# An output stage that starts inside the attention stage's block, with its tiles laid over the attention stage's

## What is computed

```
x1 = x  + 0.5 * ffn(layernorm(x))          # 1024x1024 weight, bias, LoRA terms
x2 = x1 + attn(layernorm(x1))              # latent attention, 32 heads, causal
y  = x2 + 0.5 * ffn(layernorm(x2))

attn: q    = rmsnorm(x @ wq_a.T) @ wq_b.T            # 32 heads of 64 + 64 (rope)
      ckv  = x @ wkv_a.T ; k_nope, v = rmsnorm(ckv[:64]) @ wkv_b.T
      p    = softmax(q @ k.T * scale, causal)
      out  = (p @ v).reshape(T, 32*128) @ wo.T
```

## Time and profile before

| | us |
|---|---|
| median of three runs | 1931.37 |
| the profiled execution | 1932.19 |
| its span in the trace | 1930.3 |
| TensorE busy | 1807.9 (94%) |
| VectorE busy | 1231.7 (64%) |
| ScalarE busy | 999.0 (52%) |
| GpSimd busy | 871.8 (45%) |
| mean granted TensorE clock | 0.981 |

### The profile page before, as it was taken

One profiled execution on the slowest core, in us unless ns is written; L12 is line 12 of the kernel. 1 busy time (PEld: TensorE's weight loads), 2 busy tenths in 40 slices (PEclk: granted clock), 3 DMA queues, 4 the chain that ended last, 5 costly groups with the idle time before them and its releaser, 6 DMA issues. The chain is left out here.

```text
span 1930.3 us, 44295 instructions
## 1 busy us (share of the span) xinstructions
PE 1807.9 (94%) x15472; PEld 1419.5 (74%) x15472; DVE 1231.7 (64%) x2653; ACT 999.0 (52%) x2135; POOL 871.8 (45%) x641
## 2 busy tenths in 40 slices
PE   6999959899999999999999999995799999968999
PEld 3678859777777777777777777773688888857887
DVE  5555348789888898888988888885421211125453
ACT  2211047788788887888878888783411100012210
POOL 2232112377787877878778787782000000014321
PEclk9999979999999999999999999998899999989999
DMA  6542153321222212222122221211742332225321
GB/s 225 173 159 103 55 166 97 83 64 41 84 68 67 77 41 84 68 67 71 46 84 67 67 68 50 84 63 62 256 131 87 103 115 87 66 109 175 120 88 65
DMA packets 111697, 182.48 MB, mean 95 GB/s; under 512 B 27472, under 2 KB 64464, under 8 KB 109584
## 3 DMA queue, kind: packets, MB, share of 16 engines
q1 hardware_dynamic: 111632, 181.61, 29.1%
HBM read 122.06 MB, written 59.51 MB: 94 GB/s over the span
## 5 line engine op out<-in xcount | busy, mean ns | idle before, releaser
L1040 PE MATMUL psS<-keyT,q 128*128 128x512 f32 (+2 forms) x2304 | 472.2, 350 | 24.5 <-POOL q L568 14.9
L1040 PEld LDWEIGHTS psS<-keyT,q 128*128 128x128 f32 x2304 | 380.5, 189 | 118.5 <-DVE negmax L1146 41.8
L1105 ACT ACTIVATE prob<-prob,negmax 128x640 f32<-128x640 f32 (+7 forms) x512 | 392.4, 769 | 77.7 <-DVE negmax L1146 75.0
L1156 DVE STREAM_TRANSPOSE pT<-prob 128x640 f32<-128x640 f32 (+7 forms) x512 | 380.0, 762 | 66.3 <-PE psV L1057 61.7
L1146 DVE CUSTOM_DVE_ANT_0 prob<-psS,mask 128x640 f32<-128x640 f32 (+7 forms) x512 | 371.8, 742 | 20.2 <-PE psS L1040 7.3
L419 PE MATMUL f_psy<-f_weff,f_xT 128*128 128x512 f32 x1344 | 313.8, 393 | 0.0
L1368 PE MATMUL o_psy<-o_w,o_o 128*128 128x512 f32 x1344 | 304.8, 389 | 0.0
L1368 PEld LDWEIGHTS o_psy<-o_w,o_o 128*128 128x128 f32 x1344 | 252.3, 188 | 52.3
L419 PEld LDWEIGHTS f_psy<-f_weff,f_xT 128*128 128x128 f32 x1344 | 250.9, 188 | 53.9 <-issue 1.7
L1057 PE MATMUL psV<-pT,val 32*64 32x512 f32 (+3 forms) x8192 | 265.8, 408 | 6.7 <-DVE pT L1156 6.2
L1057 PEld LDWEIGHTS psV<-pT,val 32*64 32x64 f32 x8192 | 169.1, 132 | 110.8 <-issue 67.2
(11 more groups left out here) (113 smaller groups left out, 1911.1 us busy)
## 6 DMA issues: line engine op xcount, KB each, us to landing
wo<-in_wo SPq DMA_DIRECT2D x16, 1024.0 KB, 6.0
pT<-row_scales SPq DMA_DIRECT2D x128, 128.0 KB, 2.8
oT<-pT SPq DMA_DIRECT2D x64, 256.0 KB, 2.5
o_in<-oT SPq DMA_DIRECT2D x32, 512.0 KB, 5.3
f_xt<-in_x SPq DMA_DIRECT2D x16, 512.0 KB, 4.3
f_w_in<-in_w SPq DMA_DIRECT2D x16, 512.0 KB, 6.6
w_sum<-f_w_in SPq DMA_DIRECT2D x16, 512.0 KB, 5.2
x<-f_xo SPq DMA_DIRECT2D x16, 512.0 KB, 2.9
```

The source lines that it names most:

```text
L1040: ins = nc.tensor.matmul(psS[:, slot, start + x0:start + x1], q[:, e, a, t * P:(t + 1) * P], k.keyT[:, m, b * S + x0:b * S + x1], start=(i ...
L1105: nc.scalar.activation(row, row, ACT.Exp, bias=negmax[:, n % 8:n % 8 + 1], scale=-1.0, accum_out=rowsum[:, column(n, s):column(n, s) + 1]) ...
L1156: nc.vector.transpose(pT[:, n % 2, t, 0:width], prob[:, n % RING, 0:width]).then_inc(turned, 1)
```

## The change

`output_phase` is gone. Its work is in a class `Output`, whose parts are called from the attention stage's own engine programs, in the same block. Its tiles take no memory of their own: they are placed at the addresses of attention's tiles (`homes`), and it uses the PSUM tile `psS` of the scores in place of `o_psy`. Waits on the attention's semaphores guard each overlay.

```
+        spots = [("keyT", 0), ("keyT", split), ("q", 0), ("q", split)] + [("prob", split * i) for i in range(4)]
+        spots += [("pT", split * i) for i in (0, 1, 2, 3, 6, 7, 4, 5)]
+        self.w_in = [at(f"o_w_in{j}", "qnT", row * j, [P, D]) for j in range(SLOTS)]
+        self.w = [at(f"o_w{i}", home, skip, [P, 2, D], F32R) for i, (home, skip) in enumerate(spots)]
+        self.o_in = at("o_in", "wo", 0, [P, PAIRS, P])
+        self.o = [at("o_o0", "qnT", row * SLOTS, ...), at("o_o1", "val", 0, ...)]
+        self.x_in = [at("o_x_in0", "cosT", 0, [P, D]), at("o_x_in1", "sinT", 0, [P, D])]
+        self.y = [at("o_y0", "mask", 0, [P, D]), at("o_y1", "wq", 0, [P, D])]
+        self.ps = psS
...
+    def load_weights(self, sp, pairs):
+        for pair in pairs:
+            if pair >= SLOTS:
+                sp.wait_ge(self.w_lo, pair - SLOTS + 1)
+            sp.dma_start(self.w_in[pair % SLOTS][:], self.wvo_d[pair * P:(pair + 1) * P, :]).then_inc(self.w_loaded[pair % SLOTS], 16)
...
+    def weights_hi(self, nc, act, pairs):
+        for pair in pairs:
+            if pair in (0, 1, 4, 5):
+                self.outputs_hi(nc, act, pair // 4, pair // 4, pair % 2)
+            act.wait_ge(self.w_loaded[pair % SLOTS], 16 * (pair // SLOTS + 1))
+            nc.scalar.activation(self.w[pair][:, HI, :], self.w_in[pair % SLOTS][:], ACT.Copy).then_inc(self.w_hi, 1)
```

`outputs_hi`, `outputs_lo`, `weights_lo`, `load_outputs`, `tensor_steps` and the `*_steps` hold the same instructions as before on the new tiles. Where they are called:

```
@@ SyncE, after each job of SP_STEP
+                    if r.last and s == 1 and (job, n) == ("X", 0):
+                        sp.wait_ge(q_done, 4 * units)
+                        sp.wait_ge(w_stored, 16 * (units - 2))
+                        output.load_weights(sp, range(SLOTS))
+                    if r.last and s == 1 and job == "Z":
+                        sp.wait_ge(o_stored[0], 16 * (units - 1))
+                        output.load_outputs(sp, 0)
+                    if r.last and s == 1 and (job, n) == ("X", 1):
+                        output.load_weights(sp, range(SLOTS, 2 * SLOTS))
+                        sp.wait_ge(output.o_lo, 2)
+                        output.load_outputs(sp, 1)
             rounds(sp, body)
+            sp.wait_ge(w_stored, 16 * units)
+            output.load_weights(sp, range(2 * SLOTS, PAIRS))
             for ch in range(2):
-                sp.wait_ge(o_stored[ch], 16 * 2 * PAIRS)
-            sp.wait_ge(w_stored, 16 * 2 * PAIRS)
+                sp.wait_ge(o_stored[ch], 16 * units)
+            output.sync_steps(sp)
@@ TensorE
             rounds(pe, body)
+            pe.wait_ge(maxed, TILES * units)
+            output.tensor_steps(nc, pe)
@@ ScalarE
                         evict_values(r.it, n, s)
+                        if r.last and s == 1 and n == 3:
+                            output.weights_hi(nc, act, range(SLOTS))
...
             rounds(act, body)
+            act.wait_ge(turned, TILES * units)
+            output.weights_hi(nc, act, range(SLOTS, 14))
+            for ch in range(2):
+                act.wait_ge(o_stored[ch], 16 * units)
+            output.weights_hi(nc, act, range(14, PAIRS))
+            output.scalar_steps(nc, act)
@@ VectorE
                         join_values(r.it, n, s)
+                        if r.last and s == 1 and n == 3:
+                            output.weights_lo(nc, dve, range(SLOTS))
...
             rounds(dve, body)
+            output.weights_lo(nc, dve, range(SLOTS, PAIRS))
+            output.vector_steps(nc, dve)
```

More of the change, by code:

```diff
@@ L53, in __init__ @@
     def __init__(self, nc, stack):
-        self.nc, self.stack = nc, stack
+        self.nc, self.stack, self.homes = nc, stack, {}
     def sb(self, name, shape, dt=F32):
-        return self.stack.enter_context(self.nc.sbuf_tensor(name, shape, dt))
+        tile = self.stack.enter_context(self.nc.sbuf_tensor(name, shape, dt))
+        self.homes[name] = self.nc.sbuf_base - 4 * int(np.prod(shape[1:]))
+        return tile
     def ps(self, name, shape, dt=F32):
@@ L881, in attention_phase @@
+def attention_phase(nc, k, args, oT_d, rinv_d, wvo_d, v_d, src_d, dst_d):
     wn_d, wpe_d, wv_d, wo_d = args
@@ L884, in attention_phase @@
         queries, cosT, sinT, wn_in, tab_in = k.queries, k.cosT, k.sinT, k.wn_in, k.tab_in
-        wn, wpe, q, f_split, q_copied, q_lo = queries.wn, queries.wpe, queries.q, queries.f_split, queries.q_copied, queries.q_lo
+        wn, wpe, q, f_split, q_done, q_copied, q_lo = (queries.wn, queries.wpe, queries.q, queries.f_split, queries.q_done,
+                                                        queries.q_copied, queries.q_lo)
         wv = c.sb("wv", [P, 2, KVR])
@@ L904, in attention_phase @@
         w_done, w_copied, w_stored = c.sem("w_done"), c.sem("w_copied"), c.sem("w_stored")
+        output = Output(nc, c, {**k.homes, **c.homes}, psS, src_d, dst_d, oT_d, wvo_d)
+        units = 2 * PAIRS
         block = stack.enter_context(nc.Block())
@@ L1236, in _ @@
             rounds(pool, body)
[L1240 to L1357, removed]
-                        if pair == PAIRS - 1:
-                            ins.then_inc(product, 1)
-            def step(n, j, has):
-                if has(0) and later(n, 2):
-                    pe.wait_ge(o_lo, n * 2 + 2)
-                    pe.wait_ge(result, n * 2 - 2)
-                    for half in range(2):
-                        for pair in range(PAIRS):
-                            for i, (a, m) in enumerate(PASSES):
-                                ins = nc.tensor.matmul(psy[:, j, half, :], o[:, j, a, pair, :], w[:, m, pair, half * BANK:(half + 1) * BANK],
-                                                       start=(pair == 0 and i == 0), stop=(pair == PAIRS - 1 and i == 2))
-                        ins.then_inc(product, 1)
-            output_steps(pe, step)
@@ L1400, in macaron_block @@
             k.keyT = ci.sb("keyT", [P, 2, T], F32R)
-            k.queries = Queries(ci)
+            k.queries, k.homes = Queries(ci), ci.homes
             k.cosT, k.sinT = ci.sb("cosT", [P, S]), ci.sb("sinT", [P, S])
@@ L1405, in macaron_block @@
             latents_phase(nc, k, x1_d, (wa, lnw, cos, sin), (wn, wpe, cosT, sinT), v_d)
-            attention_phase(nc, k, (wn, wpe, wv, wo), oT_d, rinv_d, wvo_d, v_d)
-        output_phase(nc, x1_d, x2_d, oT_d, wvo_d)
+            attention_phase(nc, k, (wn, wpe, wv, wo), oT_d, rinv_d, wvo_d, v_d, x1_d, x2_d)
         ffn_phase(nc, "f2_", k, x2_d, out, bias, sum_d)
```

101 lines of the change are left out of this document (100 added, 1 removed).

## The result

The changed kernel takes 1928.78 us (median of 12 runs, 1927.27 to 1932.93) against 1933.04 for the one before on the same chips (12 runs, 1930.65 to 1937.14). The ratio is 0.9978, 95% interval 0.9970 to 0.9986: 4.3 us faster. Forecast were 7.6 us and 1923.8; the measured time lies above the range. 1.7 us of the distance in absolute time is the kernel before, whose median rose from 1931.37 to 1933.04 with more runs; 3.3 us are a gain forecast too large. With the median of 1931.37 that the forecast started from, the gain measured would have given 1927.1.

What follows compares the result with a forecast made beforehand. TensorE was taken as the bound, with a serial chain before the output stage: 13.0 us earlier start, 10.3 left after pair 4's wait, 7.6 after the clock's fall; 1931.37 - 7.6 = 1923.8 us, range 1918.8 to 1927.5.

Steps and rivals of the forecast that it cites:

- Early loads: Output stage's first loads: four weights issued from about 1324.7, then tile 0, all landed by 1336.3, 4.7 us before ScalarE asks.
- Rival 4: SyncE's line: X1's store waits behind 3 MB of loads and delays later loads, slower, up to 1944.9 us; chance 0.03.
- First product: Start of the output stage: TensorE starts at 1345.6 instead of 1358.62, 13.0 us earlier.
- Tile 1 holds pair 4: Output stage: pair 4 waits for tile 1's later load and starts at 1358.9, stall 5.0 us, gain left 10.3 us.
- Rival 2: Tile 1 lands later still, after 7.8 us, pair 4 starts at 1361.9: 4.6 us off, 1926.8 us; chance 0.12.
- The clock: TensorE's clock falls again in the stall before pair 4, costing 2.7 us and leaving a gain of 7.6 us.
- Nothing lost later: From pair 4 on everything keeps its distance to TensorE: put at 0, bounds +-0.5 us.
- Rival 3: Tile 1 lands quickly (4.1 us) and the clock holds, pair 4 at 1358.2: 11.0 us off, 1920.4 us; chance 0.06.

Runs made afterwards that it cites:

- e6: The changed kernel without the early loads (pairs 0 to 3 and tile 0 issued behind X1): 1940.52 us, ratio 1.0035 to the kernel before.
- e3: The changed kernel with GpSimd's two multiplications of the last unit held until VectorE has split pair 3: 1926.05 us, ratio 0.9955 to the kernel before.
- e1: The changed kernel with tile 1's loads issued behind pair 4's load instead of pair 7's: 1919.42 us, ratio 0.9919 to the kernel before.
- e2: The changed kernel with the last unit's two stores of results issued behind pair 8's load: 1928.82 us, ratio 0.9970 to the kernel before.
- e7: The changed kernel with the edits of e1 and e3 together: 1921.64 us, ratio 0.9928 to the kernel before.
- e5: The changed kernel with 32 added matmuls behind the last V product and 38 ahead of pair 4: 1926.55 us, ratio 0.9961 to the kernel before.
- e10: e1 unchanged, profiled once more, one execution: 1919.14 us.

## Why the prediction was off

Mechanism and sign were right, two sizes were not: the time to the first product and, above all, tile 1's landing. Together they cost 4.7 us of bridge. By luck 1.9 of that is hidden: the V product was 0.7 shorter than in the first profile, which no edit touches, and the second fall of the clock 1.2 cheaper than put. That leaves the 2.9 us by which the bridge missed. The bridge, step by step:

| step | before | forecast | after |
|---|---|---|---|
| last V product | 10.83 | 10.83 | 10.16 |
| its end to the first product | 19.66 | 6.64 | 7.76 |
| first product to pair 4 | 10.62 | 13.3 | 16.90 |
| pair 4 to tile 2 | 38.20 | 40.9 | 39.72 |
| sum | 79.31 | 71.7 | 74.54 |

- **Early loads: right.** Issued at 1326.7 less 1.9 of later start, landed before ScalarE asked. e6 shows that they are the gain. The margin was smaller than put: tile 0's halves took 9.9 and 11.0 us to land, the last at 1340.9, 14.2 us after the first issue and not 11.6; ScalarE asked for them at 1342.16 and 1344.05.
- **Rival 4, X1 behind the loads: there, and hidden.** Store to loads took 6.80 us instead of 2.22, done at 1341.4, 6.4 us before SyncE had anything else to do.
- **First product: 1.1 us short.** I took VectorE's subtractions at the 1.16 to 1.23 us of the earlier trace rows, where GpSimd was idle. Here they lie beside its multiplications, and both slow each other (e3). I had not looked for which engine is busy beside a step that is moved. The Trainium skill (SBUF — State Buffer, SBUF: two separate sides) says that a VectorE operation with two inputs in SBUF and a GpSimd operation reading SBUF can't run at once, the later one waits. By that rule the trace agrees in the main: 2.29 us is 1.07 more than 1.22, where one multiplication alone is 1.30.
- **Tile 1 holds pair 4: the failed step is its size.** Issue to landing was put at 4.1 to 5.4 us, read from the earlier trace rows, where nothing lay in front of the loads, "or a little later"; with three weight loads in front it was 7.42 (e1, e2, e7). That is 2.5 of the 3.6 us; 0.8 is the later issue, of VectorE's second long subtraction, and 0.3 the copies and splits. Rival 2 had this case, at 12%: its landing of 7.8 us and its time of 1926.8 are nearest to what came.
- **The clock: right that it falls, too dear for this trace.** 1.6 us (e5), not 2.7. I priced the fall by the whole first start; how long the slow part lasts varies, and 2.7 is within what this stage shows (in e3 the 168 matmuls took 40.94 to tile 2, 2.7 more than the 38.20 of before): 5.5 us at 1358.62 in the earlier trace rows, 3.2 us at pair 4 of after, as its windows show (columns of the earlier trace rows):
```profile
1367.00:1368.00 1.00, 1.00 (x4) 0.71 (x4) 1.00 (x1) 0.03 (x1) 0.00 (x0) 0.50 0.59 238
1368.00:1369.00 1.00, 1.00 (x6) 0.83 (x5) 1.00 (x2) 0.57 (x1) 0.00 (x0) 0.93 0.82 107
```
  The time from TensorE's stop to the fall varies too. It was 4.7 us twice in the earlier trace rows; in after TensorE stopped at 1355.66 and the clock had fallen 2.3 us later:
```profile
1357.00:1358.00 1.00, 0.00 (x0) 0.00 (x0) 0.00 (x0) 0.00 (x0) 0.00 (x0) 0.95 0.89 328
1358.00:1359.00 1.00, 0.00 (x0) 0.00 (x0) 0.00 (x0) 0.00 (x0) 0.00 (x0) 0.50 1.12 342
```
  And the rule I drew from the earlier trace rows, 2.29 holds and 4.7 falls, was one trace's luck: over the same stall the clock fell when the kernel ran again (2.70), and it fell with stalls of 2.19 and 2.54 in e1 and e10. The sentence of the Trainium skill (TensorE: Matmul & The Clock Gate, Part 1) on a monitor that runs free of the program agrees with that.
- **Nothing lost later: right**, the end of the output stage keeps its distance (tile 2 at -2.88, the last product -2.9).
- **Small slips in the sums.** Rival 3's 1920.4 less 1.3 is 1919.1 and not 1918.8, the range's lower end; the middle of 1358.2 and 1359.8 is 1359.0 and not 1358.9. Neither bears on the result.

## What to carry to other kernels

When a serial wait is shortened, follow the next item in the in-order queue: here the gain of 12 us at the first product was more than half given back, mostly because one load (tile 1) stood behind loads whose slots free later, and ScalarE took it ahead of a weight that had long landed. Order DMA issues by when their buffers come free and who asks first, and take a load's time from a row with the same amount queued ahead. Check which engine runs beside every step that moves.

## What was not expected of the hardware

- VectorE subtractions from two SBUF tiles (128x1024) took 2.29 us beside GpSimd's 128x512 multiplications and 1.22 alone; GpSimd's took 2.13 to 2.25 and 1.30 to 1.34.
- With a stall of 2.19 us of TensorE its clock fell to 1.2 GHz in one trace, with 2.29 it did not in another; in the kernel before, run again, the fall came 0.9 us after TensorE had started again.
- Behind 2 MB of weight loads, SyncE's issue of tile 0's two loads took 3.98 us instead of 1.03 (3.49 of it the second alone), and behind all 3 MB that of four small stores 3.19 instead of 1.30: issuing itself slowed when much was queued. The DMA engines' share was 1.03 from 1330 to 1334.
